# Who splits the layers' weights: GpSimd whenever it may, or ScalarE and VectorE at fixed places of a step

## The chip, the core and the metric

The kernel runs on one core of a Trainium2 chip. The metric is the device time of one execution in microseconds (us); less is better. A core has a matrix engine (TensorE, PE in the profile), a vector engine (VectorE, DVE), an engine for activation functions (ScalarE, ACT), a general one (GpSimd, POOL) and a queue that issues transfers (SyncE, SP). Each takes its own instructions in order; semaphores order them among each other.

## The reference

The input is x of 2 x 2048 rows of 128 numbers. It goes through eight layers of linear attention with a feed-forward part, and then through a small mixture of four experts. A layer is, shortened:

```python
q, k, v = x @ Wq + bq, x @ Wk + bk, x @ Wv + bv          # 128 -> 128 each
Q, K = elu(q) + 1, elu(k) + 1
KV, Ksum = sum(K * v over rows), sum(K over rows)
V = Q * KV / (Q * Ksum + 1e-6)
x = layernorm(gelu(V @ Wo + bo) + x) * ln1_s + ln1_b
h = gelu(x @ Wf1 + bf1)                                  # 128 -> 512
x = layernorm(gelu(h @ Wf2 + bf2) + x) * ln2_s + ln2_b
```

After the layers comes x = layernorm(x + layers(x)); then each row is routed to two of four experts (softmax of h_norm @ router_w, hidden size 256, a layer norm inside), the two outputs are mixed and normed, and x = layernorm(x + mixed).

## The kernel before, in words

Activations lie turned, features on the 128 partitions and rows along the free axis. The 4096 rows are cut into four units of two chunks of 512 rows; eight layers times four units give 32 units (`UNITS`), numbered through. `run(step)` goes through steps s = 0 to 34. In step s every engine does, interleaved by a written order, the attention of unit s, the feed-forward part of unit s - 1, the last part of unit s - 2 (and the second chunk of unit s - 3), and the projections of unit s + 1. So each engine has its own list of some 30 to 80 instructions per step, and the places of the instructions in these lists are what this case is about. After step 34 the mixture of experts runs (`run_moe`).

Products that need more than the rounded precision are made of three passes of TensorE with rounded operands (type fp32r): high weight by high data, high by low, low by high (`product`). For that each layer's Wq, Wk, Wv (128x384, tiles `wqkv_h`, `wqkv_l`) and Wf1 (128x512, tiles `wf1_h`, `wf1_l`; the profile writes wf_h and wf_l) must be split: the high part is a rounded copy, the low part the raw weight less the high part. The tiles are double, by the layer's parity. All raw weights lie in `wraw`, loaded at the start, layer after layer.

Layer 0's weights are split by VectorE (`split_qkv_first`, `split_f_first`). The weights of layers 1 to 7 are split by GpSimd in `split_weights(l)` (L1561 to L1576): rounded copy and subtraction of Wq, Wk, Wv (L1566, L1568), as soon as TensorE has done the last projections of layer l - 2, which is in step 4(l - 1) - 2 (step 1 for layer 2), and of Wf1 (L1574, L1576), as soon as TensorE has done the last hidden product of layer l - 2, which is in step 4(l - 1). They are used from step 4l - 1 (`project`) and step 4l + 1 (`hidden`) on.

After them GpSimd prepares the experts in `prepare()`: clears `std_parts`, spreads `rn_b`, centres the experts' first weights w1 (128x1024, L1587), splits the router's weights (128x4), scales w1 (L1594), copies the bias rows in high and low (L1598, L1601) and splits w1 (L1607, L1609). It starts when six transfers have landed that SyncE issues after the last use of layer 4's weights (they overwrite the first layers' part of `wraw`). VectorE's part of it, `prepare_mean` (L1184 to L1189: a 128x1024 row sum and two small instructions), stands at the start of step 26 (`s == UNITS - 6`).

In a step of VectorE the order around the change is: at the end `low_y(1, s - 1, 0)` (L1132), and at the start of the next `normalise(1, s - 3, 1)` (L1154), `high(1, ...)` (L1167), `min_k` (L1062), `low(1, ...)` (L1177), `make_k` (L1069), `normalise(0, s - 1, 0)`, `k_by_v` (L1078), `min_k`, `high(0, s - 1, 0)` (L1170), `make_k`, `k_by_v`, and `low(0, s - 1, 0)` (L1177). On ScalarE, in the second half of a step after the table load of L613, come `gelu_hidden(s - 1, 0)`, `gelu_feed(s - 2, 1)`, `gelu_hidden(s - 1, 1..3)` (L477), and then `gelu_attend(s, 0)` and `gelu_attend(s, 1)` (L471), followed by `gelu_hidden(s - 1, 4)`, for whose end TensorE's `hidden(s - 1, 6)` waits. The logarithm and exponential of unit s (`log_z`, `exp_z`, L437 and L442) stand ahead of the table load, and at another place in odd steps than in even ones.

Of the kernel before, what the change touches and what calls it, by code (L numbers as in the profile page):

```python
# [38 lines left out]
def build(nc, x_in, w_in, par_in, const_in, w1_in, w2_in, moe_in, row_in, bias_in, out):  # L39
    with ExitStack() as ctx:  # L40
# [60 lines left out]
        on_g = raw_part(7 * EW, P)  # L101
        on_b = raw_part(7 * EW + P, P)
        w1_h, w1_l = xr_h[:, 0:EW], xr_l[:, 0:EW]
        gram_h, gram_l = xr_h[:, EW:EW + CH], xr_l[:, EW:EW + CH]

# [22 lines left out]
        rn_b_all = raw_part(7 * EW + 2 * P, P)  # L128
        std_parts = raw_part(7 * EW + 3 * P, TILES * SROWS)
# [231 lines left out]
        @block.sync  # L361
        def _(sp):
            sp.dma_start(wraw[:, 0:QKV], w_in[:, 0:QKV]).then_inc(wqkv_loaded, 16)
            sp.dma_start(x[:, 0:CH], x_in[:, 0:CH]).then_inc(x_loaded[0], 16)
            for c in range(1, 4):
                cols = slice(c * CH, (c + 1) * CH)
                sp.dma_start(x[:, cols], x_in[:, cols]).then_inc(x_loaded[c], 16)
            sp.dma_start(wraw[:, QKV:WCOLS], w_in[:, QKV:WCOLS]).then_inc(wfirst_loaded, 16)
            for c in range(4, 8):
                cols = slice(c * CH, (c + 1) * CH)  # L370
                sp.dma_start(x[:, cols], x_in[:, cols]).then_inc(x_loaded[c], 16)
            for l in range(1, LAYERS):
                cols = slice(l * WCOLS, (l + 1) * WCOLS)
                sp.dma_start(wraw[:, cols], w_in[:, cols]).then_inc(wrest_loaded[l - 1], 16)


            last = 5 * 4 - 1
            sp.wait_ge(wqkv_set, 5)
            sp.wait_ge(wf_set, 5)
            sp.wait_ge(wo_mm, upto(last, 1))  # L380
            sp.wait_ge(wf2_mm, upto(last, 1))
            sp.dma_start(w1, w1_in).then_inc(moe_loaded, 16)
            sp.dma_start(w2, w2_in).then_inc(moe_loaded, 16)
            sp.dma_start(g_all, row_in[0:1, 0:EW].to_broadcast([P, EW])).then_inc(moe_loaded, 16)
            sp.dma_start(b_raw, bias_in).then_inc(moe_loaded, 16)
            sp.dma_start(wraw[:, 7 * EW:7 * EW + 2 * P],
                         row_in[0:1, EW:].to_broadcast([P, 2 * P])).then_inc(moe_loaded, 16)
            sp.dma_start(moe_small[:, :], moe_in).then_inc(moe_loaded, 16)
# [12 lines left out]

        @block.scalar
        def _(act):
# [76 lines left out]
            def gelu_feed(u, h):  # L480
                act.wait_ge(wf2_mm, upto(u, h))
                if h == 1:
                    after(act, sql_done[1], u)
                else:
                    after(act, var_mm[1], upto(u - 1, 0))
                nc.scalar.activation(y[1][:, half(h)], O[h][:, :], GELU,  # L486
                                     bias=param(u // 4, BF2)).then_inc(gelu_done[1], 1)

            def prepare():

# [78 lines left out]
            def step(s, p, attends, feeds, ends, closes):  # L569
# [100 lines left out]
        def _(pe):  # L670
# [147 lines left out]


            def prepare_turned(s):  # L820
                pe.wait_ge(w1c_set, 1)
                pe.wait_ge(hid_done, hid_upto(s - 2, 7))
                for m in range(HB):
                    mm = nc.tensor.transpose(R[m // 4][:, tile(m % 4)], w1c[:, tile(m)], ident)
# [207 lines left out]
        def _(dve):  # L1032
# [12 lines left out]
            def split_f_first():  # L1045
# [3 lines left out]
                nc.vector.tensor_tensor(wf1_l[0][:, :], raw(0, WF1, FB * P), wf1_h[0][:, :].bitcast(F32),  # L1049
                                        ALU.subtract).then_inc(wf_set, 1)  # L1050

            def split_first(c):

                u, h = c // 2, c % 2
# [125 lines left out]
                                               op1=ALU.subtract).then_inc(xl_done[which], 1)  # L1180

            def prepare_mean():
                dve.wait_ge(moe_loaded, 16 * 6)
                nc.vector.tensor_scalar(rw, moe_small[:, 2:2 + EXPERTS], moe_small[:, 0:1], None,  # L1184
                                        ALU.mult).then_inc(prep, 1)
                nc.vector.tensor_reduce(w1_mean, w1.rearrange("p (e h) -> p e h", e=EXPERTS), AX.X,
# [227 lines left out]
                    left = [sequence for sequence in left if next(sequence, ended) is not ended]  # L1414

            def step(s, p, attends, feeds, ends, closes):
                if s == UNITS - 6:
                    prepare_mean()
                if closes:
                    normalise(1, s - 3, 1)  # L1420
# [129 lines left out]
        def _(pool):  # L1550
# [10 lines left out]
            def split_weights(l):  # L1561

                pool.wait_ge(wrest_loaded[l - 1], 16)
                if l >= 2:
                    pool.wait_ge(kvq_mm, 3 * upto(4 * (l - 2) + 3, 1))
                nc.gpsimd.tensor_copy(wqkv_h[l % 2][:, :], raw(l, 0, QKV)).then_inc(wqkv_high, 1)  # L1566
                pool.wait_ge(wqkv_high, l + 1)
                nc.gpsimd.tensor_tensor(wqkv_l[l % 2][:, :], raw(l, 0, QKV), wqkv_h[l % 2][:, :].bitcast(F32),  # L1568
                                        ALU.subtract).then_inc(wqkv_set, 1)
                if l >= 2:  # L1570
                    pool.wait_ge(wf1_mm, hid_upto(4 * (l - 2) + 3, 2 * FB - 1))
                else:
                    pool.wait_ge(wf_high, 1)
                nc.gpsimd.tensor_copy(wf1_h[l % 2][:, :], raw(l, WF1, FB * P)).then_inc(wf_high, 1)  # L1574
                pool.wait_ge(wf_high, l + 1)
                nc.gpsimd.tensor_tensor(wf1_l[l % 2][:, :], raw(l, WF1, FB * P), wf1_h[l % 2][:, :].bitcast(F32),  # L1576
                                        ALU.subtract).then_inc(wf_set, 1)

            EH = "p (e h) -> p e h"

            def prepare():

                pool.wait_ge(moe_loaded, 16 * 6)
                nc.gpsimd.memset(std_parts, 0.0).then_inc(zeros_set, 1)
                nc.gpsimd.tensor_copy(rn_b_all, moe_small[:, 1:2].to_broadcast([P, P])).then_inc(rn_b_set, 1)
                pool.wait_ge(prep, 3)
                nc.gpsimd.tensor_tensor(w1c.rearrange(EH, e=EXPERTS), w1.rearrange(EH, e=EXPERTS),  # L1587
                                        w1_mean.unsqueeze(2).to_broadcast([P, EXPERTS, H]),
                                        ALU.subtract).then_inc(w1c_set, 1)
# [3 lines left out]
                pool.wait_ge(w1c_set, 1)  # L1593
                nc.gpsimd.tensor_tensor(w1, w1c, g_all, ALU.mult).then_inc(w1c_set, 1)  # L1594
# [4 lines left out]
                for n in range(2):  # L1599
                    pool.wait_ge(b_set, 2 + n)  # L1600
                    nc.gpsimd.tensor_tensor(b_all[n][LOW_ROWS, :], b_raw[LOW_ROWS, half(n)],  # L1601
                                            b_all[n][LOW_ROWS, :].bitcast(F32), ALU.subtract).then_inc(b_set, 1)
                pool.wait_ge(b_set, 4)

                pool.wait_ge(kvq_mm, 3 * upto(UNITS - 2, 1))
                pool.wait_ge(w1c_set, 2)
                nc.gpsimd.tensor_copy(w1_h, w1).then_inc(w1_set, 1)  # L1607
                pool.wait_ge(w1_set, 1)
# [23 lines left out]

            def add_on_b(it, k):
                n = upto_chunk(it, k)
                pool.wait_ge(moe_loaded, 16 * 6)
# [62 lines left out]
```

## Time and profile before

| | |
|---|---|
| median of 3 runs | 1067.29 us (1066.52 to 1068.6) |
| the profiled execution's own time | 1066.67 us |
| its span, first to last instruction | 1064.6 us |
| PE busy | 962.3 us, 90% |
| DVE busy | 897.9 us, 84% |
| ACT busy | 830.1 us, 78% |
| POOL busy | 113.3 us, 11% |
| granted TensorE clock, mean | 0.975 |
| table loads of ACT (L570, L613) | 35 and 34, 1283 ns each |

Busy is the time in which an engine ran an instruction of the program; idle time of an engine that is not on the path costs nothing. The shares are means over all stages: in the steps of the layers (about 60 to 790 us) three engines are nearly always busy, in the experts' part after 850 us they are not. A step can be timed by a mark that occurs once in it: here the start of ScalarE's table load of L613, which stands in the middle of each step. "A to B" of two such marks is the time that one step's worth of work took.

### The profile page before, as it was taken

Reading aid. Unit: us, or ns where it says so; the run is one execution under the profiler, and the core shown is the slowest. Engines: PE = TensorE matmul, PEld = TensorE weight load, DVE = VectorE, ACT = ScalarE, POOL = GpSimd, SP = SyncE. Lnnn points to the kernel's source line nnn. Section 1 sums busy time; section 2 is a strip of 40 time slices with the busy share of each in tenths; the row PEclk is TensorE's granted clock in tenths of the full one; section 3 lists DMA queues with packets and bytes.
Section 4 is the critical chain, followed back from the end, with each engine's and each line's share of the span. In section 5 each row is a group of like instructions: output and inputs, shape, how many; then the busy total and the mean of one; then the engine's idle time right before and its main releaser. Section 6 shows DMA issues by size and latency. Waiting matters only on the chain. (4 is left out here: it accounts for less than half of the span.)

```text
span 1064.6 us, 13367 instructions
## 1 busy us (share of the span) xinstructions
PE 962.3 (90%) x3621; PEld 610.6 (57%) x3621; DVE 897.9 (84%) x2312; ACT 830.1 (78%) x1336; POOL 113.3 (11%) x111
## 2 busy tenths in 40 slices
PE   5799999999999999999999999998998469999993
PEld 3555555555555555555555555555555157787772
DVE  6769999999999999999999999999976457788864
ACT  4689999989999999999899998998888424544452
POOL 3200000000000000000000002003000012422333
PEclk9999999999999999999999999999999769999997
DMA  8000000000000000000020000000001000000000
GB/s 323 1 0 1 1 1 1 0 1 1 1 0 1 1 1 0 1 1 1 1 84 1 1 1 1 1 1 1 1 13 67 0 0 2 11 11 12 11 21 20
DMA packets 8185, 15.86 MB, mean 15 GB/s; under 512 B 945, under 2 KB 5425, under 8 KB 7985
## 3 DMA queue, kind: packets, MB, share of 16 engines
q1 hardware_dynamic: 7680, 14.82, 3.9%
q8 instruction: 31, 0.51, 0.2%
q14 instruction: 42, 0.34, 0.1%
q10 hardware_dynamic: 432, 0.20, 0.1%
HBM read 12.92 MB, written 2.10 MB: 14 GB/s over the span
## 5 line engine op out<-in xcount | busy, mean ns | idle before, releaser
L477 ACT ACTIVATE hid<-R,par 128x512 f32<-128x512 f32 x224 | 148.5, 698 | 15.5 <-PE R L677 13.6
L777 PE MATMUL Oa<-hid,wraw 128*128 128x512 f32 x256 | 133.5, 604 | 1.2
L777 PE MATMUL Ob<-hid,wraw 128*128 128x512 f32 x256 | 131.4, 596 | 0.0
L675 PE MATMUL R<-x_h,wf_h 128*128 128x512 f32 x224 | 105.7, 472 | 0.9 <-ACT hid L477 0.9
L675 PE MATMUL R<-xr_h,wqkv_h 128*128 128x512 f32 x160 | 87.6, 548 | 17.0 <-DVE cen L1506 10.3
L1121 DVE SCALAR_TENSOR_TENSOR y<-x,par,y 128x512 f32<-128x512 f32 x120 | 87.4, 747 | 11.4 <-ACT y L486 11.0
L458 ACT ACTIVATE rs<-SV,eps_ln 128x512 f32<-128x512 f32 x128 | 88.3, 690 | 10.1 <-PE SV L815 7.3
L1132 DVE TENSOR_TENSOR y_l<-y,y_h 128x512 fp32r<-128x512 f32 x128 | 94.5, 738 | 1.2
L677 PE MATMUL R<-x_h,wf_l 128*128 128x512 f32 x224 | 87.9, 393 | 0.0
L676 PE MATMUL R<-x_l,wf_h 128*128 128x512 f32 x224 | 87.9, 392 | 0.0
L463 ACT ACTIVATE rs<-rs 128x512 f32<-128x512 f32 x128 | 80.7, 630 | 1.2
L815 PE MATMUL SV<-y,mean_all 128*128 128x512 f32 x128 | 66.8, 603 | 2.9 <-ACT y L447 2.1
L777 PEld LDWEIGHTS Oa<-hid,wraw 128*128 128x128 f32 x256 | 45.9, 188 | 34.8 <-ACT hid L477 25.1
L675 PEld LDWEIGHTS R<-x_h,wf_h 128*128 128x128 f32 x224 | 42.0, 187 | 41.5 <-issue 35.2
L777 PEld LDWEIGHTS Ob<-hid,wraw 128*128 128x128 f32 x256 | 48.6, 190 | 26.7 <-issue 18.8
L677 PE MATMUL R<-xr_h,wqkv_l 128*128 128x512 f32 x160 | 63.7, 398 | 0.0
L676 PE MATMUL R<-xr_l,wqkv_h 128*128 128x512 f32 x160 | 63.5, 397 | 0.0
L675 PEld LDWEIGHTS R<-xr_h,wqkv_h 128*128 128x128 f32 x160 | 30.5, 191 | 57.5 <-DVE xr_l L1177 30.5
L1108 DVE SCALAR_TENSOR_TENSOR V<-Q,kv,rz 128x512 f32<-128x512 f32 x64 | 46.5, 748 | 19.8 <-ACT rz L442 19.8
L1128 DVE CAST y_h<-y 128x512 fp32r<-128x512 f32 x128 | 54.4, 425 | 8.8 <-PE R L794 6.6
L548 ACT ACTIVATE reluq<-V,rz 128x128 f32<-128x128 f32 x32 | 13.2, 483 | 60.3 <-DVE rz L1405 44.5
L447 ACT ACTIVATE y<-Ca 128x512 f32<-128x512 f32 x64 | 38.1, 595 | 27.8 <-PE Ca L794 27.6
(215 smaller groups left out, 2457.0 us busy)
## 6 DMA issues: line engine op xcount, KB each, us to landing
wraw<-w_dram SPq DMA_DIRECT2D x7, 768.0 KB, 11.7
x<-x_dram SPq DMA_DIRECT2D x8, 256.0 KB, 5.8
Q<-x_dram SPq DMA_DIRECT2D x1, 2048.0 KB, 7.6
out_dram<-reluq SPq DMA_DIRECT2D x8, 256.0 KB, 2.3
wraw<-w_dram SPq DMA_DIRECT2D x2, 512.0 KB, 4.0
wraw<-w_dram SPq DMA_DIRECT2D x1, 576.0 KB, 6.2
wraw<-row_dram SPq DMA_DIRECT2D x1, 512.0 KB, 5.3
wraw<-bias_dram SPq DMA_DIRECT2D x1, 512.0 KB, 6.2
```

The costliest lines, as they stand in the source:

```text
L458: nc.scalar.activation(rs[:, half(h)], SV[:, :], ACT.Ln, bias=eps_ln[:, :]).then_inc(ln_done[which], 1)
L463: nc.scalar.activation(rs[:, half(h)], rs[:, half(h)], ACT.Exp, scale=-0.5).then_inc(rs_done[which], 1)
L477: nc.scalar.activation(hid[:, m * CH:(m + 1) * CH], HIDDEN[m][:, :], GELU, bias=param(u // 4, BF1 + m % FB)).then_inc(hid_done, 1)
L675: nc.tensor.matmul(bank, w_h, a_h, start=True, stop=False)
L676: nc.tensor.matmul(bank, w_h, a_l, start=False, stop=False)
L677: return nc.tensor.matmul(bank, w_l, a_h, start=False, stop=True)
L777: mm = nc.tensor.matmul(O[h][:, :], raw(u // 4, WF2 + j * P, P), hid[:, m * CH:(m + 1) * CH], start=(j == 0), stop=(j == FB - 1))
L815: mm = nc.tensor.matmul(SV[:, :], mean_all[:, :], y[which][:, half(h)], start=True, stop=True)
L1108: nc.vector.scalar_tensor_tensor(out=V[:, half(h)], in0=Q[:, chunk(u, h)], scalar=kv[:, b:b + 1], in1=rz[:, half(h)], op0=ALU.mult, op1=AL ...
L1121: nc.vector.scalar_tensor_tensor(out=g, in0=t, scalar=b, in1=g, op0=ALU.add, op1=ALU.add).then_inc(y_done[which], 1)
L1128: nc.vector.tensor_copy(y_h[:, half(h)], y[which][:, half(h)]).then_inc(yh_done[which], 1)
L1132: nc.vector.tensor_tensor(y_l[:, half(h)], y[which][:, half(h)], y_h[:, half(h)].bitcast(F32), ALU.subtract).then_inc(yl_done[which], 1)
```

## The change

ScalarE makes the rounded copies of layers 1 to 7 and VectorE the subtractions. Layer l's high Wq, Wk, Wv come in step 4(l - 1), its high Wf1 in step 4(l - 1) + 2, each between `gelu_hidden(s - 1, 3)` and `gelu_attend(s, 0)`. The low parts come in steps 4(l - 1) + 1 and 4(l - 1) + 3, as VectorE's last instruction of the step. GpSimd splits no weights of layers any more.

The experts' preparation stays on GpSimd, but is cut into pieces, each tied to a step and to a place of VectorE's order: within a step GpSimd waits for `low(1, s - 3, 1)` ahead of the bias copies, and for `high(0, s - 1, 0)` ahead of the others. w1's centring and scaling are cut in two halves. SyncE issues five of the loads after layer 3 instead of layer 4, in another order, and only the row of `on_g`, `on_b` after layer 4, under a semaphore of its own; `on_g`, `on_b`, `rn_b_all` and `std_parts` lie 1024 columns further to the front of `wraw`. `prepare_mean` moves from step 26 to step 20.

```diff
 # SyncE
-            last = 5 * 4 - 1
-            sp.wait_ge(wqkv_set, 5)
-            sp.wait_ge(wf_set, 5)
-            sp.wait_ge(wo_mm, upto(last, 1))
-            sp.wait_ge(wf2_mm, upto(last, 1))
+            def wait_for_layer(l):
+                last = 4 * l + 3
+                sp.wait_ge(wqkv_set, l + 1)
+                sp.wait_ge(wf_set, l + 1)
+                sp.wait_ge(wo_mm, upto(last, 1))
+                sp.wait_ge(wf2_mm, upto(last, 1))
+            wait_for_layer(3)
...
+            wait_for_layer(4)
+            sp.dma_start(wraw[:, 6 * EW:6 * EW + 2 * P],
+                         row_in[0:1, EW:].to_broadcast([P, 2 * P])).then_inc(on_loaded, 16)
 # ScalarE
+            def high_weights(l, part):
+                if part == 0:
+                    act.wait_ge(wrest_loaded[l - 1], 16)
+                    if l >= 2:
+                        act.wait_ge(kvq_mm, 3 * upto(4 * (l - 2) + 3, 1))
+                    nc.scalar.activation(wqkv_h[l % 2][:, :], raw(l, 0, QKV), ACT.Copy).then_inc(wqkv_high, 1)
+                else:
+                    if l >= 2:
+                        act.wait_ge(wf1_mm, hid_upto(4 * (l - 2) + 3, 2 * FB - 1))
+                    else:
+                        act.wait_ge(wf_high, 1)
+                    nc.scalar.activation(wf1_h[l % 2][:, :], raw(l, WF1, FB * P), ACT.Copy).then_inc(wf_high, 1)
...
                     gelu_hidden(s - 1, 3)
+                if s < UNITS - 4 and s % 2 == 0:
+                    high_weights(s // 4 + 1, s % 4)
                 if attends:
                     gelu_attend(s, 0)
 # TensorE
-                pe.wait_ge(w1c_set, 1)
+                pe.wait_ge(w1c_set, 2)
 # VectorE
+            def low_weights(l, part):
+                if part == 1:
+                    dve.wait_ge(wqkv_high, l + 1)
+                    nc.vector.tensor_tensor(wqkv_l[l % 2][:, :], raw(l, 0, QKV), wqkv_h[l % 2][:, :].bitcast(F32),
+                                            ALU.subtract).then_inc(wqkv_set, 1)
+                else:
+                    dve.wait_ge(wf_high, l + 1)
+                    nc.vector.tensor_tensor(wf1_l[l % 2][:, :], raw(l, WF1, FB * P), wf1_h[l % 2][:, :].bitcast(F32),
+                                            ALU.subtract).then_inc(wf_set, 1)
...
-                if s == UNITS - 6:
+                if s == UNITS - 12:
                     prepare_mean()
...
                     low_y(1, s - 1, 0)
+                if s < UNITS - 4 and s % 2 == 1:
+                    low_weights(s // 4 + 1, s % 4)
 # GpSimd
             for c in range(8):
                 low_first(c)
-            for l in range(1, LAYERS):
-                split_weights(l)
-            prepare()
+            run(step)
...
+            def step(s, p, attends, feeds, ends, closes):
+                if 3 <= s < UNITS - 1:
+                    pool.wait_ge(xl_done[1], upto(s - 3, 1))
+                if s == UNITS - 3:
+                    high_bias()
+                if s == UNITS - 2:
+                    low_bias(1)
+                if UNITS - 11 <= s < UNITS:
+                    pool.wait_ge(xh_done[0], upto(s - 1, 0))
+                if s in (UNITS - 11, UNITS - 10):
+                    centre_w1(s - (UNITS - 11))
+                if s == UNITS - 9:
+                    set_zeros_and_rn_b()
+                if s == UNITS - 8:
+                    split_rw()
+                if s in (UNITS - 7, UNITS - 6):
+                    scale_w1(s - (UNITS - 7))
+                if s == UNITS - 3:
+                    low_bias(0)
+                if s == UNITS - 2:
+                    high_w1()
+                if s == UNITS - 1:
+                    low_w1()
```

`centre_w1(n)` and `scale_w1(n)` are the old instructions on half n (128x512); `set_zeros_and_rn_b`, `split_rw`, `high_bias`, `low_bias`, `high_w1` and `low_w1` hold the old instructions of `prepare` with their waits.

## Rows read from the trace of the kernel before

**Rows 1.** Stretches: window, length, busy us (instructions) of PE, PEld, DVE, ACT, POOL, PEclk, DMA.
```profile
100.00:640.00 540.00, 522.73 (x1708) 307.98 (x1707) 504.61 (x967) 500.02 (x769) 19.79 (x24) 1.00 0.01 5
```
**Rows 2.** Stretches from one table load of L613 to the next, one step each.
```profile
75.60:99.41 23.81, 23.00 (x76) 13.40 (x75) 21.00 (x40) 22.70 (x36) 0.00 (x0) 1.00 0.00 1
124.04:149.38 25.34, 23.48 (x77) 13.54 (x76) 23.90 (x43) 22.80 (x35) 1.93 (x2) 1.00 0.00 0
174.06:197.86 23.80, 23.60 (x79) 14.02 (x79) 22.38 (x43) 22.68 (x36) 0.00 (x0) 1.00 0.00 1
197.86:222.51 24.65, 24.43 (x83) 14.60 (x82) 22.59 (x46) 22.89 (x36) 0.00 (x0) 1.00 0.00 1
641.52:668.39 26.87, 24.71 (x83) 14.59 (x82) 25.18 (x49) 22.95 (x36) 5.33 (x4) 1.00 0.00 0
716.83:743.25 26.42, 23.97 (x76) 13.25 (x75) 25.65 (x41) 23.18 (x36) 7.74 (x6) 1.00 0.00 1
743.25:769.40 26.15, 24.93 (x84) 14.84 (x83) 24.33 (x48) 23.14 (x36) 1.13 (x2) 1.00 0.00 1
```
**Rows 3.** A group by line of GpSimd: count, busy us, mean ns, idle before.
```profile
L1576 POOL TENSOR_TENSOR wf_l<-wraw,wf_h 128x512 fp32r<-128x512 f32 x7 | 9.2, 1317 | 0.6
```
**Rows 4.** VectorE in time order (start, duration, instruction), with GpSimd's Wf1 split.
```profile
132.39 0.88 DVE L1139 CAST sq_h<-y 128x512 fp32r<-128x512 f32 x1
133.19 1.75 DVE L1132 TENSOR_TENSOR y_l<-y,y_h 128x512 fp32r<-128x512 f32 x1
```
**Rows 5.** VectorE in time order, the same place of a step without GpSimd.
```profile
182.42 0.42 DVE L1139 CAST sq_h<-y 128x512 fp32r<-128x512 f32 x1
182.75 0.68 DVE L1132 TENSOR_TENSOR y_l<-y,y_h 128x512 fp32r<-128x512 f32 x1
```
**Rows 6.** VectorE in time order, beside GpSimd's split of Wq, Wk, Wv.
```profile
169.89 0.75 DVE L1078 SCALAR_TENSOR_TENSOR Kt<-R,par,Kt 128x512 f32<-128x512 f32 x1 [0.38 <-PE R L677]
...
170.82 1.29 DVE L1177 SCALAR_TENSOR_TENSOR x_l<-x,par,x_h 128x512 fp32r<-128x512 f32 x1
...
174.07 1.41 DVE L1108 SCALAR_TENSOR_TENSOR V<-Q,kv,rz 128x512 f32<-128x512 f32 x2 [0.44 <-ACT rz L442]
```
**Rows 7.** VectorE in time order, into step 26, beside GpSimd's preparation of the experts.
```profile
655.04 0.68 DVE L1132 TENSOR_TENSOR y_l<-y,y_h 128x512 fp32r<-128x512 f32 x1
655.65 0.22 DVE L1184 TENSOR_SCALAR prep_small<-moe_small 128x4 f32<-128x4 f32 x1
...
657.10 0.74 DVE L1154 SCALAR_TENSOR_TENSOR x<-R,par,rs 128x512 f32<-128x512 f32 x1
657.88 1.57 DVE L1167 TENSOR_SCALAR xr_h<-x,par 128x512 fp32r<-128x512 f32 x1
```
**Rows 8.** VectorE in time order, beside GpSimd's bias copies and w1 split.
```profile
727.00 3.44 DVE L1144 TENSOR_TENSOR sq_l<-y,sq_h 128x512 fp32r<-128x512 f32 x2
...
741.50 2.63 DVE L1092 TENSOR_SCALAR expq<-expq 128x512 f32<-128x512 f32 x1
```
**Rows 9.** VectorE in time order, behind GpSimd's first splits.
```profile
29.12 0.72 DVE L1062 TENSOR_SCALAR expk<-expk 128x512 f32<-128x512 f32 x1
```
**Rows 10.** ScalarE in time order, two activations between tiles in SBUF, 512 and 1024 wide.
```profile
172.46 0.62 ACT L463 ACTIVATE rs<-rs 128x512 f32<-128x512 f32 x1
172.99 1.05 ACT L442 ACTIVATE rz<-rz 128x1024 f32<-128x1024 f32 x1
```
**Rows 11.** ScalarE in time order, behind the place of the rounded copies.
```profile
179.35 0.73 ACT L477 ACTIVATE hid<-R,par 128x512 f32<-128x512 f32 x1
180.45 1.44 ACT L477 ACTIVATE hid<-R,par 128x512 f32<-128x512 f32 x2 [0.36 <-PE R L677]
```
**Rows 12.** TensorE in time order, the hidden product that waits for it.
```profile
180.25 0.45 PE L675 MATMUL R<-x_h,wf_h 128*128 128x512 f32 x1
```
**Rows 13.** VectorE in time order, from the end of an odd step into the next.
```profile
211.39 0.68 DVE L1132 TENSOR_TENSOR y_l<-y,y_h 128x512 fp32r<-128x512 f32 x1
212.32 0.75 DVE L1154 SCALAR_TENSOR_TENSOR x<-R,par,rs 128x512 f32<-128x512 f32 x1 [0.25 <-ACT rs L463]
```

More of the change, by code:

```diff
@@ L100, in build @@
         b_raw = raw_part(5 * EW, EW)
-        on_g = raw_part(7 * EW, P)
-        on_b = raw_part(7 * EW + P, P)
+        on_g = raw_part(6 * EW, P)
+        on_b = raw_part(6 * EW + P, P)
         w1_h, w1_l = xr_h[:, 0:EW], xr_l[:, 0:EW]
@@ L127, in build @@
         masks = sb("masks", [P, 2 * EXPERTS * EXPERTS])
-        rn_b_all = raw_part(7 * EW + 2 * P, P)
-        std_parts = raw_part(7 * EW + 3 * P, TILES * SROWS)
+        rn_b_all = raw_part(6 * EW + 2 * P, P)
+        std_parts = raw_part(6 * EW + 3 * P, TILES * SROWS)
         prep_small = sb("prep_small", [P, 3 * EXPERTS])
@@ L224, in build @@
         moe_loaded = sem("moe_loaded")
+        on_loaded = sem("on_loaded")
         x0_loaded = sem("x0_loaded")
@@ L374, in _ @@
                 sp.dma_start(wraw[:, cols], w_in[:, cols]).then_inc(wrest_loaded[l - 1], 16)
-            last = 5 * 4 - 1
-            sp.wait_ge(wqkv_set, 5)
-            sp.wait_ge(wf_set, 5)
-            sp.wait_ge(wo_mm, upto(last, 1))
-            sp.wait_ge(wf2_mm, upto(last, 1))
+            def wait_for_layer(l):
[5 more added lines that the diff above has]
+            wait_for_layer(3)
             sp.dma_start(w1, w1_in).then_inc(moe_loaded, 16)
+            sp.dma_start(g_all, row_in[0:1, 0:EW].to_broadcast([P, EW])).then_inc(moe_loaded, 16)
+            sp.dma_start(moe_small[:, :], moe_in).then_inc(moe_loaded, 16)
+            sp.dma_start(b_raw, bias_in).then_inc(moe_loaded, 16)
             sp.dma_start(w2, w2_in).then_inc(moe_loaded, 16)
[L384 to L388, printed above, removed]
+            wait_for_layer(4)
+            sp.dma_start(wraw[:, 6 * EW:6 * EW + 2 * P],
+                         row_in[0:1, EW:].to_broadcast([P, 2 * P])).then_inc(on_loaded, 16)
             sp.wait_ge(V_done, 2 * UNITS)
@@ L1182, in prepare_mean @@
             def prepare_mean():
-                dve.wait_ge(moe_loaded, 16 * 6)
+                dve.wait_ge(moe_loaded, 16 * 5)
                 nc.vector.tensor_scalar(rw, moe_small[:, 2:2 + EXPERTS], moe_small[:, 0:1], None,
@@ L1559, in low_first @@
                                         ALU.subtract).then_inc(first_low, 1)
[L1561 to L1577, printed above, removed]
@@ L1579, in _, with two_experts, centre_w1 @@
-            EH = "p (e h) -> p e h"
-            def prepare():
-                pool.wait_ge(moe_loaded, 16 * 6)
+            def two_experts(w, n):
+                return w[:, half(n)].rearrange("p (e h) -> p e h", e=2)
+            def centre_w1(n):
+                pool.wait_ge(prep, 3)
+                nc.gpsimd.tensor_tensor(two_experts(w1c, n), two_experts(w1, n),
+                                        w1_mean[:, 2 * n:2 * n + 2].unsqueeze(2).to_broadcast([P, 2, H]),
+                                        ALU.subtract).then_inc(w1c_set, 1)
@@ L1584, in prepare, with set_zeros_and_rn_b, split_rw @@
+            def set_zeros_and_rn_b():
+                pool.wait_ge(moe_loaded, 16 * 5)
+                pool.wait_ge(on_loaded, 16)
                 nc.gpsimd.memset(std_parts, 0.0).then_inc(zeros_set, 1)
                 nc.gpsimd.tensor_copy(rn_b_all, moe_small[:, 1:2].to_broadcast([P, P])).then_inc(rn_b_set, 1)
[L1586 to L1589, printed above, removed]
+            def split_rw():
@@ L1592, in prepare, with scale_w1, high_bias @@
                 nc.gpsimd.tensor_tensor(rw_l[:, :], rw, rw_h[:, :].bitcast(F32), ALU.subtract).then_inc(rw_set, 1)
-                pool.wait_ge(w1c_set, 1)
-                nc.gpsimd.tensor_tensor(w1, w1c, g_all, ALU.mult).then_inc(w1c_set, 1)
+            def scale_w1(n):
+                pool.wait_ge(w1c_set, 1 + n)
+                nc.gpsimd.tensor_tensor(w1[:, half(n)], w1c[:, half(n)], g_all[:, half(n)],
+                                        ALU.mult).then_inc(w1c_set, 1)
+            def high_bias():
                 pool.wait_ge(wf1_mm, hid_upto(4 * 6 + 3, 2 * FB - 1))
@@ L1598, in prepare, with low_bias, high_w1, low_w1 @@
                     nc.gpsimd.tensor_copy(b_all[n][:, :], b_raw[:, half(n)]).then_inc(b_set, 1)
[L1599 to L1602, printed above, removed]
+            def low_bias(n):
+                pool.wait_ge(b_set, 2 + n)
+                nc.gpsimd.tensor_tensor(b_all[n][LOW_ROWS, :], b_raw[LOW_ROWS, half(n)],
+                                        b_all[n][LOW_ROWS, :].bitcast(F32), ALU.subtract).then_inc(b_set, 1)
+            def high_w1():
                 pool.wait_ge(b_set, 4)
                 pool.wait_ge(kvq_mm, 3 * upto(UNITS - 2, 1))
-                pool.wait_ge(w1c_set, 2)
+                pool.wait_ge(w1c_set, 4)
                 nc.gpsimd.tensor_copy(w1_h, w1).then_inc(w1_set, 1)
+            def low_w1():
                 pool.wait_ge(w1_set, 1)
@@ L1634, in add_on_b @@
                 n = upto_chunk(it, k)
-                pool.wait_ge(moe_loaded, 16 * 6)
                 pool.wait_ge(xt_done, n * TILES)
```

## The prediction

> **What bounds the kernel now.** I read the busy shares first, then the stretches, then the time line of VectorE, ScalarE and GpSimd, and the waits in it. In 540 us of the layers' stage PE is busy 523 us, DVE 505 and ACT 500, POOL 20 [rows 1]. No engine alone is the bound: three run in lockstep at 97%, 93% and 93%, each waiting for the others by tenths of a microsecond. So a delay on any of them moves everything behind it unless it falls where that engine was about to wait. GpSimd, nearly idle, can only matter through what it does to others.
>
> The stretches show what that is. One step's work from an even step's mark to the next odd one's takes 23.80 us where GpSimd is silent, and 23.81 where it is silent too, early on (75.60 to 99.41). The stretch 124.04 to 149.38, with GpSimd's Wf1 split in it, takes 25.34: 1.54 more [rows 2]. Stretches from an odd mark to an even one take 24.65. The time line says why: there the cast of sq_h takes 0.88 and y_l 1.75 us [rows 4], against 0.42 and 0.68 [rows 5], that is 0.46 + 1.07 = 1.53 more, the whole difference. GpSimd's subtraction lasts 1.32 [rows 3]; VectorE's instruction stands still until it is over. It is not so everywhere: beside GpSimd's copy of Wq, Wk, Wv VectorE's Kt, with one input from PSUM, takes its 0.75, and x_l 1.29 instead of some 0.74, but behind it VectorE still waits 0.44 us for rz, so that this delay is free [rows 6].
>
> The page SBUF — State Buffer of the Trainium skill, section Who interferes with whom, says that VectorE's two-port forms, and its forms with two SBUF inputs against a reading GpSimd, take a port pair in turns with GpSimd, whole instructions at a time, while forms with at most one SBUF input outside those modes are untouched. The rows agree on both sides.
>
> **What goes.** (a) Six Wf1 splits (layers 2 to 7; layer 1's ran at the start) at 1.54: 9.2 us. (b) Step 26: its stretch takes 26.87, 2.22 above 24.65 [rows 2]. VectorE's `prepare_mean` starts 655.65 and the next instruction 657.10, 1.45 later [rows 7]; that part moves to step 20 and stays. Without it `normalise` stood 0.93 behind y_l [rows 13], here 2.06 [rows 7]: 1.13 is its cost. xr_h with 1.57, behind GpSimd's centring of w1, holds the other 1.09. This goes. (c) The stretch from step 28's mark, with the bias copies: 26.42 less 23.80 is 2.62 [rows 2]; two sq_l take 3.44 there [rows 8]. (d) The next, with w1's split: 26.15 less 24.65 is 1.50 [rows 2], expq with 2.63 [rows 8]. (e) At the start expk takes 0.72 behind GpSimd's first split; a one-input instruction of this width takes 0.42 [rows 5, 9]. I take 0.3 for it; bounds 0 and 1.6, if a second stall of the length of the subtraction [rows 3] counts too (I leave it out, as VectorE then waits for ScalarE's logarithms). Together 9.2 + 1.1 + 2.6 + 1.5 + 0.3 = 14.7 us, if the pieces of the experts' preparation collide with nothing at their new places.
>
> They are put where VectorE has instructions with an input from PSUM ahead: behind `low(1, ...)` come make_k, normalise and k_by_v, some two microseconds at 0.75 each less their overlap [rows 6]; behind `high(0, ...)` make_k and k_by_v, some 1.7 with the wait of 0.38 between. Halves of w1's two instructions fit if a half takes about what the 128x512 subtraction takes, 1.32 [rows 3], and the bias pieces are of that size. The one that doesn't, low_w1 of 1024 columns in step 31, meets a VectorE that is about to wait for the Gram matrix. Cost 0; without that cover at most the 5.2 of (b) to (d) returns. The loads are issued a layer earlier, with three steps to spare before step 20; the queues are otherwise idle (DMA share 0.01 [rows 1]). Cost 0. If they came late, VectorE would stand at the start of step 20 with all engines behind it.
>
> **What comes on ScalarE.** The trace has no ACT Copy from SBUF in this stage. The nearest row is the 512-wide activation between SBUF tiles: 0.62 long, the next one starting 0.53 after it; the 1024-wide one takes 1.05, so 0.84 ns a column, and 384 columns cost 0.53 - 0.11 = 0.42 [rows 10]. Bounds: the streaming alone, 0.43 and 0.32, and the whole duration, 0.62 and 0.51. Is anything there to hide it? `gelu_attend(s, 0)` and (s, 1) and hidden 4 start behind one another. Hidden 4 ends 180.08 [rows 11], and TensorE's hidden product 6 starts 180.25 [rows 12]: it waits for it. Behind it TensorE runs without a gap, and ScalarE and VectorE wait for its centring. ScalarE's own wait of 0.36 [rows 11] takes up the delay of one instruction, not TensorE's. So each copy costs its full 0.53 or 0.42. Layer 1's first falls in step 0, where ScalarE has no hidden GELUs and waits for TensorE's attention product (if that cover is gone, 0.4 more): 7 x 0.53 + 6 x 0.42 = 6.2 us (all bounds: 4.9 to 7.4). Behind ScalarE's added waits (weights loaded, last use of the buffer) stand both attention GELUs; the awaited work is one to two steps old, cost 0.
>
> A page speaks for a worse case. Between the engines' two sets of functions each step already loads tables, 1.28 us each. ScalarE: Activation LUTs, section Table sets, of the Trainium skill says that a function outside the loaded set needs a load, and that copy is in every set. No row here has a Copy under the GELU set; by the first half alone each of the 14 would bring two loads (the third rival), by the second none, which I follow.
>
> **What comes on VectorE.** Subtraction of two SBUF tiles, 512 wide: the next instruction starts 0.61 after it (655.04 to 655.65 [rows 7]); 384 wide 0.61 less a quarter of nearly all of it, 0.47 (bounds 0.46 and 0.61). At an odd step's end `normalise` starts 0.93 behind y_l because it waits for rs [rows 13]; 0.93 - 0.61 = 0.32 is free. So 0.29 for each of 7 Wf1 parts, 0.15 for each of 7 others: 3.1 us. Behind it nothing hides more: `prepare_mean` stood at this very place and cost 1.45 - 0.32 = 1.13, which, with xr_h's stall, is all of that stretch's excess. In step 20 the free 0.32 is already used by layer 5's Wf1 part in front, so `prepare_mean` costs 0.3 more there. Bounds: 0, if like x_l in [rows 6] it dies in a later wait, and 7.6, with nothing free. The awaited copy is a step old; cost of the wait 0. It can't be below nothing, as no engine waits for less by it.
>
> **The sum.** -14.7 + 6.2 + 3.1 + 0.3 = -5.1 us. Against the profiled execution's own time of 1066.67 (2.07 more than the span, for what lies around it) 1061.6. The median shown, 1067.29, is 0.6 above that execution, so I forecast 1062.1 as the median of a few runs.
>
> **Rivals.** First, absorbed: the inserted instructions partly fall into others' waits. VectorE's waits in a step (0.25, 0.4, 0.4 to 1.0 us for rs, R and rz) speak for it; `prepare_mean`, not absorbed at all, speaks against. VectorE's part for nothing and ScalarE's at the lower bound give 14.7 - 4.9 - 0.3 = 9.5 off: 1057.7.
>
> Second, no slack: both engines' parts cost from start to start or more, and the free 0.32 isn't there, since ScalarE's copy has shifted the waits. 14.7 less 7.4, 7.6 and 0.3 leaves the sum at +0.6: 1067.9, no measurable change. That the three engines are at 93% and more speaks for it; that all later instructions shift by the same amount, so that the waits stay, against.
>
> Third, slower: Copy isn't in the GELU set, each copy is followed by a reload. Place: in front of `gelu_attend(s, 0)`; price 2 x 1.28 x 14 = 35.8: about 1098. It decides from three copies on (3 x 2.57 is over 5.1 by more than 2.1), so it is all or nothing. ScalarE's Square and the Copy of the Gram part run without loads of their own (69 loads in 35 steps), which speaks against.
>
> Fourth, slower as well: the 1.54 belongs to something else that comes once in four steps, a change of layer, and stays. Then -5.1 + 9.2 = +4.1: 1071.4. Against it: step 4's stretch differs by just VectorE's two long instructions, and the stretch at 75.60, of the same place, is 23.81.
>
> **Chances.** Forecast (1059 to 1065) 0.66, absorbed 0.15, no slack 0.12, table loads 0.03, something else 0.04. A measurement of this kernel can tell about 0.2%, 2.1 us, from no change. Faster by more: the forecast nearly whole, and absorbed: 0.80. Within: no slack and the forecast's upper edge, 0.13. Slower: 0.07. The range reaches into the first two rivals, 1056.5 to 1066.5.
>
> **What would show it.** Right: no y_l of 1.75 in the page's groups (mean of y_l near 690 ns instead of 738); stretches without GpSimd's stalls, those with a copy 23.80 + 0.5 or 24.65 + 0.2 or so, in no place 25.3; ACT Copy between hidden and attend with about 0.51 and 0.62 us; still 69 table loads in the steps; GpSimd's pieces beside make_k and k_by_v, these unchanged. Wrong: stretches of the layers' steps 23.8 and 24.65 in spite of the copies (absorbed), or 24.5 and 25.2 (no slack); xr_h or expk stretched beside GpSimd's new pieces; a wait of VectorE for GpSimd's or SyncE's loads in step 20.

## The result, and the profile after

The changed kernel takes 1060.08 us (median of 4 runs, 1059.94 to 1060.35), the kernel before beside it 1066.97 (4 runs, 1066.52 to 1068.6): ratio 0.9933, interval 0.9916 to 0.995, 6.9 us less. The forecast was 1062.1, 5.1 less. The profiled execution took 1059.94, its span from first to last instruction is 1057.9 (before 1066.67 and 1064.6: 6.7 less).

| busy us | PE | DVE | ACT | POOL |
|---|---|---|---|---|
| before | 962.3 | 897.9 | 830.1 | 113.3 |
| after | 964.9 | 888.0 | 835.3 | 86.9 |

VectorE has 14 instructions more and is busy 10 us less: the time that its instructions no longer stand still beside GpSimd's is more than the work it got.

The stretches of one step's work of the kernel after, from mark to mark (ScalarE's table load, L633 here and L613 before), with the columns of [rows 2]:

```profile
75.18:99.52 24.34, 23.19 (x76) 13.37 (x75) 21.08 (x40) 23.13 (x36) 0.00 (x0) 1.00 0.00 1
124.45:148.67 24.22, 23.52 (x77) 13.55 (x76) 22.47 (x43) 23.07 (x37) 0.00 (x0) 1.00 0.00 0
173.44:197.78 24.34, 23.51 (x77) 13.56 (x76) 22.48 (x43) 23.12 (x37) 0.00 (x0) 1.00 0.00 1
197.78:222.68 24.90, 24.61 (x83) 14.55 (x82) 23.09 (x47) 22.94 (x35) 0.00 (x0) 1.00 0.00 1
492.79:519.13 26.34, 24.63 (x83) 14.58 (x82) 24.50 (x50) 22.94 (x36) 0.00 (x0) 1.00 0.00 1
641.57:666.31 24.74, 24.49 (x82) 14.53 (x82) 22.94 (x47) 22.94 (x35) 1.29 (x1) 1.00 0.00 0
715.55:739.37 23.82, 23.36 (x77) 13.57 (x76) 22.39 (x43) 22.70 (x35) 2.46 (x3) 1.00 0.00 0
739.37:764.03 24.66, 24.44 (x83) 14.59 (x82) 22.59 (x46) 22.91 (x36) 2.32 (x2) 1.00 0.01 1
764.03:788.44 24.41, 22.25 (x84) 12.76 (x83) 21.19 (x33) 20.60 (x32) 2.83 (x2) 1.00 0.00 1
```

Line against line with [rows 2]: 23.81 has become 24.34, a Wf1 copy of ScalarE (+0.53). 25.34 is 24.22: the stall beside GpSimd's split has gone (-1.54) and the smaller copy has come (+0.42). 23.80 is 24.34, a Wf1 copy again, and 24.65 is 24.90, VectorE's Wf1 part (+0.25; 0.25 to 0.30 in four other layers). The fifth line is step 20, to which `prepare_mean` has moved: 26.34, where it took 24.67 before. 26.87, 26.42 and 26.15 are 24.74, 23.82 and 24.66: the experts' preparation on GpSimd, 2.46 and 2.32 us busy in the last two, costs nothing more. The ninth line, 24.41, has no counterpart in [rows 2]; the same stretch of the kernel before took 25.40, and further down is why the change did not cause that.

The page's group of y_l has a mean of 685 ns (738 before). What was added, in the groups of ScalarE and VectorE (columns as in [rows 3]):

```profile
L507 ACT ACTIVATE wf_h<-wraw 128x512 fp32r<-128x512 f32 x7 | 4.6, 655 | 0.0
L501 ACT ACTIVATE wqkv_h<-wraw 128x384 fp32r<-128x384 f32 x7 | 3.8, 544 | 0.0
```
```profile
L1081 DVE TENSOR_TENSOR wf_l<-wraw,wf_h 128x512 fp32r<-128x512 f32 x7 | 4.8, 684 | 0.0
L1077 DVE TENSOR_TENSOR wqkv_l<-wraw,wqkv_h 128x384 fp32r<-128x384 f32 x7 | 3.8, 549 | 0.0
```

ScalarE's time line in the middle of step 6, TensorE's hidden product 6 there, and VectorE's time line at the end of step 7 (start, duration, instruction):

```profile
177.60 0.66 ACT L507 ACTIVATE wf_h<-wraw 128x512 fp32r<-128x512 f32 x1
178.13 0.71 ACT L477 ACTIVATE y<-Cb,par 128x512 f32<-128x512 f32 x1
...
179.27 1.31 ACT L483 ACTIVATE hid<-R,par 128x512 f32<-128x512 f32 x2
181.11 0.69 ACT L483 ACTIVATE hid<-R,par 128x512 f32<-128x512 f32 x1 [0.53 <-PE R L699]
```
```profile
180.14 0.47 PE L697 MATMUL R<-x_h,wf_h 128*128 128x512 f32 x1 [0.34 <-ACT hid L483]
```
```profile
211.30 0.68 DVE L1164 TENSOR_TENSOR y_l<-y,y_h 128x512 fp32r<-128x512 f32 x1
211.90 0.68 DVE L1081 TENSOR_TENSOR wf_l<-wraw,wf_h 128x512 fp32r<-128x512 f32 x1
212.50 0.74 DVE L1186 SCALAR_TENSOR_TENSOR x<-R,par,rs 128x512 f32<-128x512 f32 x1
```

The copy takes 0.53 us of ScalarE's list, with no table load beside it. Behind it the two hidden GELUs run on without the wait of [rows 11]; that wait, 0.36, did take up ScalarE's delay there. But TensorE's hidden product 6 starts 6.70 us behind the mark (173.44) instead of 6.19 (180.25 [rows 12] behind 174.06), and has waited 0.34 for ScalarE. ScalarE's next hidden GELU is idle for 0.53 ahead of it where it waited for nothing before: what is won in one wait is lost in the next, and the step is longer by the whole copy. On VectorE the wait of 0.25 for rs [rows 13] is gone, and x starts 1.20 behind y_l instead of 0.93.

### The profile page after: what moved, and what is told of

It reads as the page before. It is cut to its first block and busy times, and to the rows that moved or that the text cites. A ratio compares the mean times of both kernels' runs of the same rounds, so it can differ in the third digit from the quotient of the medians.

```text
span 1057.9 us, 13392 instructions
## 1 busy us (share of the span) xinstructions
PE 964.9 (91%) x3621; PEld 609.9 (58%) x3621; DVE 888.0 (84%) x2326; ACT 835.3 (79%) x1350; POOL 86.9 (8%) x85
## 5 line engine op out<-in xcount | busy, mean ns | idle before, releaser
L1164 DVE TENSOR_TENSOR y_l<-y,y_h 128x512 fp32r<-128x512 f32 x128 | 87.7, 685 | 1.2
```

The lines of the kernel that those rows point to most:

```text
L1164: nc.vector.tensor_tensor(y_l[:, half(h)], y[which][:, half(h)], y_h[:, half(h)].bitcast(F32), ALU.subtract).then_inc(yl_done[which], 1)
```

## The experiments

A ratio is against the kernel before on the same chip. Stretches are named by the step whose mark ends them: "step 5" is what was 25.34 in [rows 2]. The edits are shown abridged: definitions, removals that go without saying and repeated lines are left out.

**One half of the change at a time.** e1_weights_only: the kernel before with the weights moved, the experts' preparation left.

```diff
+                if s < UNITS - 4 and s % 2 == 0:
+                    high_weights(s // 4 + 1, s % 4)
+                if s < UNITS - 4 and s % 2 == 1:
+                    low_weights(s // 4 + 1, s % 4)
-            for l in range(1, LAYERS):
-                split_weights(l)
             prepare()
```

> The kernel before with the layers' weights alone moved (ScalarE copies, VectorE subtracts, at the places of the changed kernel); the experts' preparation stays as before. My theory: gains and costs add up. Gone: six stalls of 1.54 us and 0.3 at the start, 9.5; new: 7 x 0.53 and 6 x 0.42 on ScalarE, 7 x 0.28 and 6 x 0.13 on VectorE, 8.9. So about -0.6 us against the kernel before, 1066.4: this half of the change brings nothing. Rival (moving the weights off GpSimd is what brings the 6.9 us, the pieces of the preparation little): 1060 to 1062.

Measured: ratio 1.0, 0.999 to 1.001 (1066.42, the kernel before 1066.32). Steps 3, 5 and 8 take 24.34, 24.23 and 24.91 as in the changed kernel, step 29 stays at 26.41. Step 26 takes 27.30, 0.43 more than before: VectorE's added part now stands ahead of `prepare_mean` and uses the wait that hid 0.32 of it. So moving the weights alone brought nothing: 9 us of stalls were exchanged for 9 us of work.

e2_prep_only: the changed kernel with GpSimd splitting the weights at the old moments (from step 21 on behind the wait for `low(1, s - 3, 1)`, too).

```diff
-                    high_weights(s // 4 + 1, s % 4)
-                    low_weights(s // 4 + 1, s % 4)
+                    # GpSimd, ahead of its waits in step s
+                    if s == (1 if l == 2 else 4 * (l - 1) - 2):
+                        split_qkv(l); split_qkv_low(l)
+                    if s == 4 * (l - 1):
+                        split_f(l); split_f_low(l)
```

> The changed kernel with the layers' weights back on GpSimd at the moments of the kernel before; the experts' preparation in pieces, loads and VectorE's sum as changed. My theory: the stalls of steps 26, 29 and 30 go, 1.1 + 2.6 + 1.5 = 5.2 us, and perhaps the 1.0 of the granted clock in step 31: 1061.8, or 1060.8 with it. Each Wf1 split stalls VectorE by 1.5 us again. Rival (as for the first run): 1066 to 1067.

Measured: 0.9935, 0.9922 to 0.9949 (1059.92, lower than both values that were expected). The Wf1 stall is back, the preparation's are gone (step 29 at 23.79):

```profile
124.15:149.47 25.32, 23.48 (x77) 13.55 (x76) 23.90 (x43) 22.80 (x35) 1.94 (x2) 1.00 0.00 0
```

In step 25 the stall is smaller (24.88 instead of 25.33), because there the split stands behind the added wait: 0.45 us of this run's gain are not the preparation's.

The two halves, ratios 1.0 and 0.9935, multiply to the whole, 0.9933, within the intervals. The rival that the weights are what brought the gain is out.

**Same engine, another place.** e3_gpsimd_at_places: nothing of the split on ScalarE and VectorE; GpSimd's instructions tied to the two places (layer 1's in steps 1 to 3).

```diff
+                    # behind low(1, s - 3, 1)
+                    if s == 4 * (l - 1):     split_qkv(l)
+                    if s == 4 * (l - 1) + 1: split_f(l)
+                    # behind high(0, s - 1, 0)
+                    if s == 4 * (l - 1):     split_qkv_low(l)
+                    if s == 4 * (l - 1) + 1: split_f_low(l)
```

> The changed kernel with the layers' weights on GpSimd, but each instruction tied to one of the two places of a step behind which VectorE's next instructions have an input from PSUM (rounded copies behind low(1, s - 3, 1), subtractions behind high(0, s - 1, 0)); nothing of them on ScalarE and VectorE. w1's scaling comes a step later. My theory (only the place of GpSimd's instruction counts, a stall arises only with VectorE's SBUF-to-SBUF instructions): all 9.0 us that the added instructions cost in the changed kernel go and no stall comes: 1051. y_l stays at 0.68, x_l at 0.74. Rival (GpSimd's reading of SBUF costs VectorE something wherever it stands): 1060 or more, with Kt, x or expk lengthened by about 1 us in the steps with a split.

Measured: 1050.94, ratio 0.9852, 0.9839 to 0.9864. GpSimd and VectorE in time order in step 5, and the stretch ending there:

```profile
139.60 0.61 POOL L1635 CAST wf_h<-wraw 128x512 fp32r<-128x512 f32 x1 [20.88 <-DVE xr_l L1183]
142.35 1.28 POOL L1639 TENSOR_TENSOR wf_l<-wraw,wf_h 128x512 fp32r<-128x512 f32 x1 [2.14 <-DVE x_h L1176]
```
```profile
142.18 0.75 DVE L1075 SCALAR_TENSOR_TENSOR Kt<-R,bias,expk 128x512 f32<-128x512 f32 x1
...
143.30 0.75 DVE L1084 SCALAR_TENSOR_TENSOR Kt<-R,par,Kt 128x512 f32<-128x512 f32 x1 [0.37 <-PE R L683]
...
143.98 0.75 DVE L1183 SCALAR_TENSOR_TENSOR x_l<-x,par,x_h 128x512 fp32r<-128x512 f32 x1
```
```profile
122.81:146.62 23.81, 23.33 (x77) 13.55 (x76) 22.39 (x43) 22.70 (x35) 1.90 (x2) 1.00 0.00 0
```

GpSimd's subtraction runs 142.35 to 143.63, beside VectorE's two Kt, each with one input from PSUM, and the wait between them, and ends 0.35 before x_l, which has two in SBUF. All take their usual time and the step is 23.81. The same two instructions of GpSimd cost 1.51 us in e2 (25.32 against 23.81). In two other steps, 2 and 21, an x_l does meet a GpSimd instruction and takes 1.2 instead of 0.75; the stretches, 22.31 and 23.81, are no longer for it. What counts is not the engine, but beside what its instruction falls.

**Same engines as changed, another place.** e4_in_waits moves both; e5_act_in_wait and e6_dve_in_wait one each.

```diff
 # ScalarE (e4, e5)
+                if s < UNITS - 4 and s % 2 == 0:
+                    high_weights(s // 4 + 1, s % 4)
                 if attends:
                     square(0, s, 0)
 # VectorE (e4, e6)
+                if s <= UNITS - 4 and s % 4 == 2:
+                    low_weights(s // 4 + 1, 1)
+                if 4 <= s <= UNITS - 4 and s % 4 == 0:
+                    low_weights(s // 4, 3)
                 if attends and s % 2 == 0:
                     attend(s, 0)
```

> The changed kernel with the same instructions on the same engines at other places: ScalarE's copies in front of square(0, s, 0) of even steps, where it waits 0.45 us for the centring, VectorE's subtractions in front of attend(s, 0) of even steps, where it waits up to 1.0 us for rz. My theory (an added instruction costs its start-to-start time less the wait at its place): ScalarE 7 x 0.08, VectorE 0; 9.0 becomes 0.6 and the time 1051.7. Rival (what was added to a 93% busy engine is paid wherever it stands): about 1060, unchanged.

> The changed kernel with ScalarE's copies alone moved to the wait in front of square(0, s, 0). My theory: a 0.53 or 0.42 us instruction in a wait of 0.45 costs 0.1 or nothing, so 6.2 us of ScalarE's cost become 0.6: 5.6 less than the changed kernel, some 8.8 + 3.6 = 12.5 below the kernel before on the same chip. Rival (the gain of the run with both moved lies in VectorE's part): less than 3 below the changed kernel.

> The changed kernel with VectorE's subtractions alone moved in front of attend(s, 0) of even steps. My theory: 7 x 0.28 and 6 x 0.13 us go, 2.8 less than the changed kernel, some 9.7 below the kernel before. Rival: ScalarE's copies have used up VectorE's wait for rz (they delay VectorE and ScalarE alike, but if rz came earlier against V, the wait is shorter), so that 1 us or nothing is won.

Measured: e4 1051.0, ratio 0.9856 (0.9843 to 0.9868); e5 1054.42, 0.988 (0.9865 to 0.9895); e6 1056.79, 0.9904 (0.9889 to 0.9918). ScalarE's time line of e4 in step 6, then VectorE's:

```profile
179.36 0.59 ACT L453 ACTIVATE y<-R 128x512 f32<-128x512 f32 x1
179.84 0.63 ACT L507 ACTIVATE wf_h<-wraw 128x512 fp32r<-128x512 f32 x1
180.39 0.60 ACT L453 ACTIVATE y<-Ca 128x512 f32<-128x512 f32 x1
```
```profile
170.18 0.49 DVE L1202 TENSOR_SCALAR x_h<-x,par 128x512 fp32r<-128x512 f32 x1
170.58 0.55 DVE L1077 TENSOR_TENSOR wqkv_l<-wraw,wqkv_h 128x384 fp32r<-128x384 f32 x1
171.65 1.42 DVE L1140 SCALAR_TENSOR_TENSOR V<-Q,kv,rz 128x512 f32<-128x512 f32 x2 [0.52 <-ACT rz L448]
```

ScalarE's copy fills the wait for the centring, and y<-Ca starts 1.03 us behind y<-R, as it does without a copy in between (181.79 and 182.82 in the kernel before); behind VectorE's part there are still 0.52 us to wait. In e4's steps 4 to 19 all stretches are 23.80 to 23.82 and 24.62 to 24.68, as if nothing had been added. e5 is 12.5 below the kernel before (expected 12.5) and e6 10.2 below (expected 9.7). The changed kernel is 6.9 below, so by these medians ScalarE's part cost about 5.6 and VectorE's 3.3, roughly two to one, as forecast. The rival that a 93% busy engine pays wherever it stands is out.

**Twice the work at the same place.** e7_act_twice and e8_dve_twice. The edit of e7 for Wf1 is shown; Wq, Wk, Wv and VectorE's subtractions in e8 are doubled the same way.

```diff
+                    act.wait_ge(wf_set, l)
+                    nc.scalar.activation(raw(l - 1, WF1, FB * P), raw(l, WF1, FB * P), ACT.Copy)
                     nc.scalar.activation(wf1_h[l % 2][:, :], raw(l, WF1, FB * P), ACT.Copy).then_inc(wf_high, 1)
```

> The changed kernel with each of ScalarE's copies made twice, the first time into a dead part of wraw (128x384 and 128x512, results unused). My theory: no wait at this place, so the second set costs as much as the first: 7 x 0.53 + 6 x 0.42 = 6.2 us more than the changed kernel, about 0.7 below the kernel before. Rival (the step's place had slack for one): more than 0.6 each, 8 us and above; or under 3, if a part falls in ScalarE's wait of 0.36 further on.

> The changed kernel with each of VectorE's subtractions made twice, the first time into a dead part of wraw. My theory: the wait of 0.32 us for rs at this place is used up by the first, so the second costs its full start-to-start time, 7 x 0.60 + 7 x 0.47 = 7.5 us, where the first cost 2.8: 0.6 above the kernel before. In the stretches 0.60 and 0.47 more each. Rival (no such wait, VectorE's work is partly hidden everywhere): again 2.8.

Measured: e7 1066.52, 0.999 (0.9981 to 1.0), 6.1 above the changed kernel by the ratios (expected 6.2). e8 1068.67, 1.0017 (1.0008 to 1.0027), 9.0 above it (expected 7.5). The stretches of steps 7 (e7) and 8 (e8), 24.34 and 24.90 in the changed kernel:

```profile
174.86:199.72 24.86, 23.50 (x77) 13.54 (x76) 22.50 (x43) 23.64 (x38) 0.00 (x0) 1.00 0.00 1
```
```profile
199.12:224.66 25.54, 24.68 (x83) 14.58 (x82) 23.69 (x48) 22.97 (x36) 0.00 (x0) 1.00 0.00 1
497.12:526.07 28.95, 26.44 (x83) 15.43 (x82) 25.17 (x51) 23.21 (x36) 0.00 (x0) 0.94 0.01 1
```

The second copy costs 0.52, like the first. The second subtraction costs 0.64 here (0.58 to 0.61 in steps 4, 12, 24 and 28) where the first cost 0.25 to 0.30: there is one wait of 0.3 us, and it is used once. e8's profile is of the slowest of its ten executions (1071.02). Its step 20 takes 28.95 with a granted clock of 0.94, 2.0 more than the 0.6 of its kind; step 22 is 0.8 over where such steps are 0.5 over, cause open. Without the 2.0, the steps from the mark of step 1 to the last are 7.5 longer than in the changed kernel, which is what was expected; why the whole times lie 9.0 apart is open.

**VectorE's sum of w1 in a wait.** e9_mean_in_wait is e3 with `prepare_mean` moved in front of `attend(s, 0)` in step 20.

> The kernel with GpSimd's splits at places, and VectorE's prepare_mean (1.45 us) of step 20 moved from the step's start to in front of attend(s, 0), where VectorE waits 0.99 us for rz. My theory: its cost falls from 1.13 to 0.46, 0.7 less than the kernel with GpSimd at places, some 16.1 below the kernel before. Rival (V's product, which TensorE awaits, is then late by all of it): 0.3 more.

Measured: 1050.14, ratio 0.9839 (0.9822 to 0.9855), the fastest here; its interval overlaps e3's, so the whole time doesn't tell the two apart. The stretches do, step 20 of e3 and steps 20 and 21 of e9:

```profile
485.68:511.43 25.75, 24.65 (x83) 14.59 (x82) 23.93 (x49) 22.92 (x35) 1.52 (x2) 1.00 0.01 2
```
```profile
485.98:510.61 24.63, 24.42 (x83) 14.59 (x82) 23.54 (x48) 22.89 (x35) 1.52 (x2) 1.00 0.01 2
510.61:534.50 23.89, 22.80 (x75) 13.16 (x74) 23.06 (x45) 22.70 (x35) 2.90 (x3) 1.00 0.01 3
```

Step 20 takes 1.1 us less, of which 0.1 comes back in the next stretch: VectorE starts V 0.45 late (511.05 against rz ready at 510.60), and hardly any of that delay reaches the other engines. `prepare_mean` costs 0.1 there; the 0.46 that I expected was too much.

**Three profiles more of unchanged kernels,** for step 31.

> The changed kernel once more, for its profile alone. Question: is the stretch of 25.4 against 24.4 us in step 31, with the clock granted at half for 3.4 us, a property of the kernel before that the change took away, or of the execution? If of the kernel, 24.4 again here; if of the execution, it may be 25.4 to 25.8 here. All other stretches as in the first profile, and step 16's 25.2 tells whether that was chance (24.9).

> The changed kernel a third time, for the same question: 24.4 us in step 31 if the clock there is the kernel's own, 25.4 or more in some execution if it isn't.

> The kernel before once more, for its profile alone: 25.4 us in step 31 if the half clock is its own, 24.4 if it is the execution's.

Measured: spans 1057.2, 1057.8 and 1065.3 (times 1059.17, 1059.75, 1067.18). The changed kernel's step 31 is 24.39 and 24.41 again, step 16 25.21 and 25.22 again. The kernel before, a second time:

```profile
770.34:794.75 24.41, 22.23 (x84) 12.76 (x83) 18.98 (x33) 20.59 (x31) 0.00 (x0) 1.00 0.00 1
640.87:669.32 28.45, 26.24 (x83) 15.43 (x82) 25.18 (x49) 23.10 (x35) 5.33 (x4) 0.94 0.00 0
```

Here its step 31 is 24.41 like the changed kernel's, and step 26, 26.87 in [rows 2], is 28.45 with a clock of 0.94. TensorE's granted clock falls to half, 1.2 GHz, for 3.4 us, and where it does so differs: in step 31 in one execution of this kernel, in step 26 in another. So the 0.99 us between 25.40 and 24.41 belongs to the execution, not to the change.

## Why the prediction was right

**What bounds the kernel.** This was right. Stalls and added work appear in the stretches at their full size unless a wait is at their place, in every one of the eleven kernels.

**What goes.** Each term came at its size, from the marks of all 34 steps of both profiles. The six Wf1 stalls of 1.54 are gone; net of the copy of 0.42 that came into the same steps the difference is -1.08 to -1.12 (forecast -1.12). Step 26 is -2.13 (forecast -2.22, and 0.15 for VectorE's part), steps 29 and 30 are -2.60 and -1.49 (2.62, 1.50). The start is -0.3 (0.30): from the start of GpSimd's last split of x to the first mark it is 8.03 and 8.01 us in the two profiles of the kernel before, and 7.71 or 7.72 in the three of the changed one. The expk of 0.72 takes 0.41 now; a second one, which took 1.49, takes 0.42, and this second stall had cost nothing, as the prediction supposed. As a whole, e3, in which nothing is added to ScalarE and VectorE, is 14.8 us ahead of the kernel before by its stretches, those with a half clock set right (forecast 14.7).

At their new places the pieces collided with nothing but one:

```profile
781.37 2.96 DVE L1209 SCALAR_TENSOR_TENSOR x_l<-x,par,x_h 128x512 fp32r<-128x512 f32 x1
784.25 0.15 DVE L1225 COPY prep_small<-R 128x4 f32<-128x4 f32 x1
785.40 0.69 DVE L1228 CAST xr_h<-Oa 128x512 fp32r<-128x512 f32 x1 [1.01 <-PE Oa L860]
```

That is VectorE in step 31 beside GpSimd's w1 split: x_l takes 2.96, and then VectorE still waits 1.01 for the Gram matrix. The forecast cover held.

**What comes.** ScalarE's copies cost 0.52 to 0.54 and 0.42 (forecast 0.53, 0.42), though a copy lasts 0.66 and 0.54, longer than the row's 0.62 and 0.51: start to start is what is paid. VectorE's parts cost 0.25 to 0.30 and 0.09 to 0.18 (0.29, 0.15), and layer 1's Wq, Wk, Wv part, in step 2, nothing; with `prepare_mean`, step 20 is 1.67 over (forecast 0.29 + 1.13 + 0.32 = 1.74).

**The sum.** -5.1 was forecast. From the mark of step 1 to that of step 33 the changed kernel's profile is 5.98 shorter. 0.99 of that is the half clock in step 31 of the one profile of before; 4.99 and the 0.3 of the start are the terms, 5.3 us. The spans differ by 6.7: a further 0.34 lies behind the last mark, in the experts' part, where spans from that mark vary from 231.0 to 232.8 us between the profiles without a change to it.

So the mechanism was right and its terms add up to within 0.2 us, but the time came out 2.0 below the forecast, 1060.08 against 1062.1. Of this 0.3 is that the kernel before measured 1066.97, not the 1067.29 from which I started. In the two profiles the rest is for the most part TensorE's clock, which I took as equal in both. For the medians, 6.9 apart, nothing here shows how much of the rest is the clock: the interval of the ratio, about 5.3 to 9.0 us, has the 5.3 of the terms at its edge. That the time stayed in the range owes something to the range's width.

One term the other way was missed: step 16 is 0.54 over instead of 0.25, in all three profiles of the changed kernel and in e1, e5 and e7, with VectorE idle for 0.33 between two sq_l:

```profile
403.58 0.69 DVE L1176 TENSOR_TENSOR sq_l<-y,sq_h 128x512 fp32r<-128x512 f32 x1
404.60 0.69 DVE L1176 TENSOR_TENSOR sq_l<-y,sq_h 128x512 fp32r<-128x512 f32 x1 [0.33 <-issue]
```

It is absent in e2, e3, e4, e6, e8 and e9, whose lists of VectorE differ ahead of it. No engine is named as the releaser; the cause is open.

**The rival of the table loads** is out: the copies ran among the GELUs with no load of their own. Between the copy at 177.60 and the GELU at 178.13 there is none, and the steps still hold 69 (35 and 34).

**The other rivals.** Absorbed, no slack and a change of layer are each out by the stretches: steps 3 and 7 with a copy take 24.34 and not 23.8, step 8 takes 24.90 and not 25.2, and step 5 without a split takes 24.22. What "no slack" says comes true in e8, when the wait has been used already.

What stays open: whether the changed kernel really meets the half clock less often in the layers' stage. Behind step 1 its three profiles have none, and the two profiles of before have one each. (Step 1, near 42 us, has one too in some executions and then takes 17.8 to 18.1 instead of 17.2: in all three of the changed kernel, in one of the two of before.) Of the experiments, e3, e4, e5 and e7 had it in step 31 (25.66 to 26.05), e8 in step 20, and e1, e2, e6 and e9 nowhere there. On one chip the runs of e1 lie from 1064.2 to 1068.85 and those of the kernel before from 1065.13 to 1069.24: several us of spread come from something that isn't in the program.

## What to carry to other kernels

When three engines run in lockstep, cost an added instruction as its start-to-start time less the wait that already stands at its place, and look for a place with a wait: the same 28 instructions cost 9 us in one order and almost nothing in another. Before moving work off GpSimd because it stalls VectorE, look at what it falls beside: tied by a semaphore to VectorE's instructions with an input from PSUM, it added nothing to the steps, kept the other engines free and was 8.6 us faster than the move (ratios 0.9852 and 0.9933). And test the halves of a change apart: here one brought all and the other nothing.

## What was not expected of the hardware

The granted clock fell to half (1.2 GHz) for 3.4 us in the middle of the layers' stage in some executions and not in others, though TensorE had done the same work up to there. The first two lines are step 31 of the kernel before, 4.8 us ahead of the fall and the 3.4 us of it; the other two are the same places in the changed kernel's step 31, where the clock stayed:

```profile
781.00:785.80 4.80, 3.39 (x16) 1.95 (x15) 4.01 (x7) 4.06 (x6) 0.00 (x0) 1.00 0.00 0
785.80:789.20 3.40, 3.40 (x6) 1.35 (x4) 1.67 (x4) 1.30 (x3) 0.00 (x0) 0.50 0.00 0
```
```profile
775.60:780.40 4.80, 3.38 (x16) 1.94 (x15) 3.96 (x7) 4.11 (x6) 0.00 (x0) 1.00 0.00 0
780.40:783.80 3.40, 2.97 (x11) 1.44 (x10) 3.33 (x3) 2.20 (x4) 2.39 (x2) 1.00 0.00 0
```

TensorE had been busy 3.39 and 3.38 of 4.8 us, with 16 products in each, and the clock fell in one and not in the other. One such stretch costs 1.0 us in step 31 of the kernel before (25.40 against 24.41), 1.2 to 1.6 in that of e3, e4, e5 and e7, and 1.6 in step 26 (28.45 against 26.87). That is as much as one of the stalls this change was about, so one profile of each kernel can mislead by that much.

The Trainium skill, page TensorE: Matmul & The Clock Gate, section Part 1: The HAM clock gate (the "warmup" mystery), says that what the gate looks at runs free and doesn't restart with a kernel, so that the moment differs by where the work happens to fall. The profiles fit this (the same work, once with the fall and once without, 25.40 and 24.41 us); no run here isolates it.
